# Graph attention and mixture of experts: the one-hot rows of the edge counts written in the order in which TensorE reads them

## The reference

```
xn = layernorm(x); h = xn @ W + b_w
e = leaky_relu(s_dst[dst] + s_src[src] + b_a);  w = exp(e)
out = segment_sum(w / denom[dst] * h[src], dst);  x = x + out
x = x + moe(layernorm(x))        # 8 experts, top 2, gelu
```

## Time and profile before

| | us |
|---|---|
| median of 3 runs | 788.67 (786.93 to 788.84) |
| profiled execution, its time | 787.67 |
| its span, first to last instruction | 786.0 |
| PE busy | 701.5 |
| DVE busy | 559.3 |
| ACT busy | 458.8 |
| POOL busy | 283.5 |

### The profile page before, as it was taken

The page is one execution under the profiler, slowest core; times in us unless marked ns, Lnnn a source line. Parts: engine busy times, 40 slices in busy tenths (PEclk is TensorE's granted clock), DMA queues, the critical chain, the costliest instruction groups (busy, mean ns, idle before and its releaser), DMA issues.

```text
span 786.0 us, 15439 instructions
## 1 busy us (share of the span) xinstructions
PE 701.5 (89%) x3556; PEld 527.0 (67%) x3557; DVE 559.3 (71%) x1520; ACT 458.8 (58%) x1226; POOL 283.5 (36%) x427
## 2 busy tenths in 40 slices
PE   3977863999899999999999999999589899999992
PEld 1855641777677776767677777776347788888881
DVE  4999977999888898879887888853495333333331
ACT  3223379778778776767676777721354455555551
POOL 3336620022222222222111222211305677777764
PEclk9888976999999999999999999999789999999998
DMA  9431000000000000000000000000793577777766
GB/s 337 158 107 55 0 1 1 15 29 28 28 27 3 28 27 28 27 28 27 28 27 28 27 12 17 27 28 28 245 407 112 103 130 133 133 128 135 135 119 80
DMA packets 28949, 59.70 MB, mean 76 GB/s; under 512 B 3664, under 2 KB 8144, under 8 KB 28624
## 3 DMA queue, kind: packets, MB, share of 16 engines
q0 software_dynamic: 10176, 24.12, 17.1%
q1 hardware_dynamic: 18704, 34.89, 12.0%
HBM read 35.93 MB, written 23.07 MB: 75 GB/s over the span
## 4 chain that ended last, share of the span: by engine, by line
PE 52%; DMA 10%; issue 5%; DVE 4%; POOL 2%; POOLq 2%; ACT 0%; DVEq 0%; ACTq 0%
PE ps L772 10%; PE ps L790 10%; PE ps L773 9%; DMA out_dram<-y,si 9%; PE ps L726 7%; PE ps L879 3%; PE ps L753 2%; PE ps L893 2%; PE ps L737 2%; PE ps L820 1%; DMA xg<-xn_table,gi 1%; PE ps L746 1%; PE ps L869 1%; PE ps L759 1%; DVE hot_r L1509 1%
## 5 line engine op out<-in xcount | busy, mean ns | idle before, releaser
L973 ACT ACTIVATE weight<-sdst_b,ss 128x125 f32 (+1 forms) x400 | 118.3, 386 | 95.5 <-DVE A_lo L1339 95.5
L772 PE MATMUL ps<-H_hi,A_hi 128*125 128x512 f32 x400 | 163.0, 408 | 0.9 <-DVE x_all L1353 0.9
L773 PE MATMUL ps<-H_lo,A_hi 128*125 128x512 f32 x400 | 157.9, 395 | 0.0
L1278 DVE TENSOR_SCALAR hot_k<-lane_k,key_t 128x250 bf16<-128x250 bf16 x600 | 120.6, 282 | 4.4 <-DVE weight_sum L1327 4.3
L524 POOL TENSOR_SCALAR seed<-seed 128x1 f32<-128x1 f32 x20 | 4.2, 210 | 330.9 <-DVE seed L1380 330.9
L982 ACT ACTIVATE weight<-weight,ss 128x125 f32<-128x125 f32 x400 | 119.8, 384 | 0.0
L790 PE MATMUL ps<-H_hi,A_lo 128*125 128x512 f32 x400 | 104.9, 402 | 0.0
L726 PE MATMUL ps<-hot_k,hot_l 128*128 128x250 bf16 x500 | 80.7, 286 | 16.0 <-DVE hot_k L1278 15.9
L772 PEld LDWEIGHTS ps<-H_hi,A_hi 128*125 128x125 f32 x400 | 74.2, 185 | 21.6 <-issue 3.7
L773 PEld LDWEIGHTS ps<-H_lo,A_hi 128*125 128x125 f32 x400 | 74.3, 186 | 16.1
L879 PE MATMUL ps<-W_e,xgT 128*128 x352 | 85.0, 385 | 0.0
(11 more groups left out here) (235 smaller groups left out, 1126.7 us busy)
## 6 DMA issues: line engine op xcount, KB each, us to landing
W_e<-in_L_ffn_W_dram SPq DMA_DIRECT2D x16, 512.0 KB, 9.3
xf<-in_x_cols_dram SPq DMA_DIRECT2D x10, 512.0 KB, 5.9
x_all<-in_x_dram SPq DMA_DIRECT2D x20, 256.0 KB, 5.8
out_dram<-x_all SPq DMA_DIRECT2D x20, 256.0 KB, 2.0
xn_table<-xn SPq DMA_DIRECT2D x20, 256.0 KB, 2.2
b_b<-in_L_ffn_b_dram SPq DMA_DIRECT2D x1, 2048.0 KB, 12.6
Wf<-in_L_gnn_W_dram SPq DMA_DIRECT2D x1, 1024.0 KB, 5.5
out_dram<-x_all POOLq DMA_DIRECT2D x4, 256.0 KB, 7.8
```

Source lines behind the costliest of these rows:

```text
L772: pe.matmul(ps_agg[0:TN, :], A_hi[:, k, :], H_hi[:, k, :], start=(k == 0), stop=False)
L773: m = pe.matmul(ps_agg[0:TN, :], A_hi[:, k, :], H_lo[:, k, :], start=False, stop=False)
L973: m = nc.scalar.activation(weight[:, s, k, :], dst_scores, ACT.Relu, bias=ss[:, 0, k:k + 1], scale=1.0 - SLOPE)
L1278: return nc.vector.tensor_scalar(into, lane_k[:, :], float(HW * h), key, ALU.add, ALU.is_equal)
```

## The change

Four edits go together.

- `hot_l` has HALVES * BASE + 1 = 31 matrices in place of 19. Matrix BASE * h + c belongs to chunk c of half h, as in `hot_k`. TensorE reads it at a fixed address and loads one word of the table instead of eleven.
- `pair_rows` is called once per half, inside `pairs_of`, right ahead of that half's three `hot_k`. It writes three matrices (384 elements) and reads the source lanes at an address from registers (`at + rel`). The one call per tile between two folds is gone.
- In steps where t is a register (those of the loop) `count` waits once, for the tenth half of the tile; in the steps written out it waits for each half as before.
- `hot_l` grows by 12 * 256 bytes per partition. To make room, small tensors of the table's setup now share places with others; their operations are the same.

```diff
-            regs = [pe.alloc_register(f"pe_word{k}") for k in range(WORDS - 1)]
+            regs = [pe.alloc_register("pe_word")]
...
-                chunk = [pe.snap(within(pe.snap(regs[h]), 0, SPAN - BASE)) for h in range(HALVES)]
                 def low_of(h, c):
-                    return hot_l[:, bass.ds(chunk[h] + c, 1), :].rearrange("p c n -> p (c n)")
+                    return hot_l[:, BASE * h + c, :]
...
+                at_once = not isinstance(t, int)
+                if at_once:
+                    pe.wait_ge(pairs_ok, HALVES * t + HALVES)
                 for h in range(HALVES):
-                    pe.wait_ge(pairs_ok, HALVES * t + h + 1)
+                    if not at_once:
+                        pe.wait_ge(pairs_ok, HALVES * t + h + 1)
...
-            def pair_rows(at):
-                shape = [P, SPAN, P // 2, 2]
+            def pair_rows(h, chunk):
+                shape = [P, BASE, P // 2, 2]
                 return nc.vector.tensor_tensor(
-                    hot_l[:, 0:SPAN, :].rearrange("p c (n j) -> p c n j", j=2),
+                    hot_l[:, BASE * h:BASE * h + BASE, :].rearrange("p c (n j) -> p c n j", j=2),
                     lane_l[:, :].rearrange("p (n j) -> p n j", j=2).unsqueeze(1).to_broadcast(shape),
-                    lo2[:, bass.ds(at, SPAN), :].unsqueeze(2).to_broadcast(shape), ALU.is_equal)
+                    lo2[:, bass.ds(chunk, BASE), :].unsqueeze(2).to_broadcast(shape), ALU.is_equal)
...
                     rel = dve.snap(within(dve.snap(regs[1 + h]), 0, SPAN - BASE))
+                    pair_rows(h, dve.snap(within(at + rel, 0, CW - BASE)))
                     for c in range(BASE):
                         m = hot(hot_k[:, BASE * h + c, :], h, key_t[:, bass.ds(rel + c, 1)])
...
                     fold(t + 1, 1 - s, 1)
-                    if has(t, -2):
-                        pair_rows(at)
                     for n in range(2, 5):
```

More of the change, by code:

```diff
@@ L120, in gnn_moe_kernel @@
         layer_end = top[0]
+        lo_n = sg("lo_n", [1, BANKS * NT, 2], F32, layer)
+        ex_n = sg("ex_n", [1, BANKS * NT, 2], F32, layer)
+        rel_n = sg("rel_n", [1, NT, HALVES], F32, layer)
+        ex_t = sg("ex_t", [1, 3, NT], F32, layer)
+        zero_t = sg("zero_t", [1, NT], F32, layer)
+        thr = sg("thr", [P, 2, 2], F32, layer)
+        found = sg("found", [P, 2, 2], F32, layer)
+        chunk_mm = sg("chunk_mm", [P, 2, CG], F32, layer)
+        layer_end = top[0]
         layer.close()
@@ L126, in gnn_moe_kernel @@
         A_lo = sg("A_lo", [P, NT, TN], F32R, first)
-        hot_l = sg("hot_l", [P, SPAN + 1, P], BF16, first)
+        hot_l = sg("hot_l", [P, HALVES * BASE + 1, P], BF16, first)
         weight_sum = sg("weight_sum", [P, 2, TN], F32, first)
@@ L131, in gnn_moe_kernel @@
         reach("stage_1_end", max(layer_end, top[0]), first)
-        chunk_mm = sg("chunk_mm", [P, 2, CG], F32, first)
         thr_i = sg("thr_i", [P, 2], I32, first)
[L134 to L140, removed]
         ss = sg("ss", [P, 2, NT], F32, first)
@@ L727, in count @@
                                   start=(h % 2 == 0 and c == 0), stop=False)
-                more = extra_in(pe, regs[HALVES])
+                more = extra_in(pe, regs[0])
                 with pe.If(more > 0):
-                    at = pe.snap(extras_before(pe, regs[HALVES]) * HALVES)
+                    at = pe.snap(extras_before(pe, regs[0]) * HALVES)
                     with pe.Fori(0, more) as n:
@@ L733, in count @@
                             pe.wait_ge(xpair_ok, at + n * HALVES + h + 1)
-                            pe.matmul(half_of(h), hot_l[:, SPAN, :], hot_k[:, HALVES * BASE, :],
+                            pe.matmul(half_of(h), hot_l[:, HALVES * BASE, :], hot_k[:, HALVES * BASE, :],
                                       start=False, stop=False).then_inc(xcount_ok, 1)
@@ L1297, in pairs_of @@
                                                     tile_key[:, bass.ds(t, 1)], None, ALU.subtract).then_inc(xkey_ok, 1)
-                            nc.vector.tensor_tensor(hot_l[:, SPAN, :], lane_l[:, :],
+                            nc.vector.tensor_tensor(hot_l[:, HALVES * BASE, :], lane_l[:, :],
                                                     lo2[:, bass.ds(chunk, 1), 0].to_broadcast([P, P]), ALU.is_equal)
@@ L1426, in _ @@
             first_at = pair_keys(0)
-            pair_rows(first_at)
             dve.wait_ge(key_ok, 1)
```

## The result

The changed kernel takes 812.11 us (median of 4 runs, 811.61 to 812.87) against 788.46 of before: ratio 1.0304, 95% interval [1.0287, 1.0322]. It is slower, as forecast, and 9 us above the 803 forecast. The stated range of 794 to 813 holds it by 0.9 us; rival 1's own range, 797 to 809, does not. The profiled execution took 811.65 us with a span of 810.0, against 787.67 and 786.0.

What follows compares the result with a forecast made beforehand. TensorE bounds the loop now, VectorE after the change (1.7 us more a tile): +6.8 ahead, +0.4 at step 3, +8.3 in the loop, -0.5 behind sum to +15.0 us on 787.67, giving 803; range 794 to 813.

Steps and rivals of the forecast that it cites:

- rival 1: Whole kernel: VectorE becomes the bound, 803 us, own range 797 to 809; chance 0.78.
- VectorE becomes the bound, so the kernel gets slower: Loop: VectorE's new round of 44.6 us exceeds TensorE's 40.6, adding 8.3 us; the kernel goes to 803.
- the room of 1.9 us a round: Loop before the change: VectorE's work and jump pause take 41.16 of 43.04 us, leaving 1.9, not 4.6.
- rival 2: Loop: VectorE's 2.9 us pause ahead of even steps is room and can shrink; 787 us, not slower; chance 0.07.
- 1.49 us a tile for ten small instructions: VectorE's pair_rows: ten instructions cost 2.75 us, the one removed saves 1.26; net +1.49 us a tile.
- The 0.18 for the fold and the address: VectorE, per tile: lost overlap between two folds, 0.08 us, plus the first new instruction's address computation, 0.1 us.
- The pause ahead of even steps, 2.9 us as before: VectorE's jump back: pause stays 2.9 us, six times 2.91 in the loop; its shrinking would prove the forecast wrong.
- I count nothing: TensorE's clock: new pauses up to 3 us in even steps priced at zero, since 2 us idle kept 2.4 GHz.
- The sum: Whole kernel: 6.8 before step 3, 0.4 there, 8.3 in the loop, -0.5 behind it; +15.0 us.
- rival 3: Loop's odd steps: the count's single wait makes weigh wait, 0.6 us in each of 7, +4: 807; chance 0.07.
- the idle ahead of odd steps: Sign in the loop's profile: VectorE's idle there, 1.66 us before, would be gone, under 0.3 us.
- The counts at 2.9 us: TensorE in the loop: 25 count matmuls fall from 4.33 (even) and 3.90 us (odd) to near 2.9.

Runs made afterwards that it cites:

- e6: The changed kernel with VectorE's loop alone written out, so without its jump back: 782.05 us, ratio 0.9923 to the kernel before.
- e7: The kernel before with VectorE's loop alone written out, so without its jump back: 788.22 us, ratio 0.9996.
- e2: The changed kernel with the reciprocal, which raises den_ok, moved ahead of the first five halves of one-hots: 786.39 us, ratio 0.9992 to the kernel before.
- e1: The changed kernel with extra, never-read matmuls filling TensorE's pause ahead of the product that waits for den_ok: 797.41 us, ratio 1.0128 to the kernel before.
- e5: The kernel before with nothing but the single wait per tile in the loop's count: 783.20 us, ratio 0.9933.
- e4: The changed kernel with TensorE computing the same hot_l addresses from registers, as before: 807.19 us, ratio 1.0266 to the kernel before.
- e3: The changed kernel with a wait for each half in the loop, as before: 807.97 us, ratio 1.0257 to the kernel before.
- e12: The kernel before with pair_rows called a second time per tile, two folds later (1.26 us more on VectorE): 819.82 us, ratio 1.0411.
- e9: The kernel before with the loops of VectorE and TensorE both written out: 771.92 us, ratio 0.9785.

## Why the prediction was right, and where it was not

- *VectorE becomes the bound, so the kernel gets slower:* right. e6 and e7 show the jump's pause as VectorE's own, and with it the room of 1.9 us a round; rival 2 falls as a whole, though the pause did shrink by 0.7 us, which the prediction had named as a sign against itself.
- *1.49 us a tile for ten small instructions:* right; 352 ns each against 359. Step 2 grew by 1.58 us (1.7 forecast), the loop's even step by 20.73 - 19.40 = 1.33 and the odd by 20.39 - 18.85 = 1.54 (L1358 to the end of the last hot_k, from 264.33, 286.77 and 309.31 less their idle). The 0.18 for the fold and the address is thus not seen in the loop. The Trainium skill's price, an estimate of 357 ns by "VectorE: DVE Perf Modes", section "The TRN2 errata — SBUF-src ops pay a fixed extra latency per instruction", is met by this trace too.
- *The pause ahead of even steps, 2.9 us as before:* too long. It is 2.2 us in five of six rounds; the jump itself is no shorter, but more work is queued when it is taken (e2). VectorE's round alone is thus 43.5 us (e1), not the 44.6 of the sum: 0.7 by the pause, and the rest by the steps, 41.1 in place of 41.65.
- *"I count nothing" for the clock:* the step that failed. The prediction saw the pauses of up to 3 us at this wait (L759, now L763), took the 2 us of step 3 as proof that the clock stays, and priced them at zero. Even these 2 us were PEld's; PE's own pause at 206.03 us was 1.52. The new pauses cost 1.8 us a round (45.26 against 43.46): 12.6 us in the loop's six waits, and 2.9 at step 3. That is 15.5, nearly all of it the clock's: e1 gave back 14, after the 1.7 that its own matmuls cost.
- *The sum:* 24.0 against 15.0. In the loop 13.2 against 8.3: 12.6 for the waits behind the slow clock, less 7 * (44.6 - 43.5) = 7.7 for VectorE's shorter round. Ahead of it 9.5 against 7.2, the difference at step 3; behind it 0.5 against -0.5; and the 0.8 of the first stage. The forecast was as near as it was because two errors in the loop had opposite signs. That is luck, and so is the place inside the range: its upper end came from rival 3, which did not happen. Of the signs that it gave for itself, the idle ahead of odd steps did not go and the pause ahead of even steps did not stay.
- *The counts at 2.9 us:* right (2.87). That fixed addresses give all of it was wrong: e5 shows that most of the gain, 0.8 of 1.45 and of 1.02 us, is the work for the waits. The prediction had the single wait down as a risk alone; on the kernel before it is a gain by itself (e5). No run has the fixed addresses with the old hot_l, since they need its new order.
- *Rival 3, weigh waits for the counts:* not in the changed kernel (the trace of the loop has no such wait), and in e4 as soon as the counts are slow.

The Trainium skill, "TensorE: Matmul & The Clock Gate", section "HAM oscillation — how this bites in real kernels", describes a like failure, with waits for DMA in the place of this wait for VectorE: pauses between groups of matmuls let the clock fall, and each group then starts at half rate. The traces agree that it happens: 0.50 behind 3.1 us of idle, 1.00 behind 0.9 us. Between these the same pause had either outcome, in the changed kernel and e3 behind 2.5 us, in e2 and e12 behind 1.5 to 2.6.

## What to carry to other kernels

When a change lengthens the engine that is not the bound, look at what the bound engine does while it waits: a wait in the middle of its work can be followed by a lower clock, as here, and the slow stretch comes back as a wait on the other side. Raise early the semaphore that such a wait stands on. And price each edit of a change alone: here one wait in place of ten gave 0.7% by itself, and with the other edits beside it the kernel was 3.0% slower.

## What the runs showed of the hardware

- A jump back cost VectorE's sequencer 2.8 to 3.1 us and TensorE's 0.2. The engine was idle for less of it where it had more work left at the branch: 2.9 us with 0.3 us of work left (before), 2.5 with 1.0 (one round of the changed kernel; 2.2 in the others), 1.1 with 2.1 (e2).
- A pause of 2.5 us once left TensorE's clock at 1.00 and once not, in the same code. In e12 it fell behind 1.50 us and stayed behind 2.39. Behind 3.0 to 3.2 us it fell each time, twelve times in the changed kernel and e3.
- 25 matmuls of 250 bf16 columns took 2.88 us with nothing in their way, 2.9 to 3.2 with one register operation each where the loop is written out (e9), 3.1 to 3.5 with it in the loop (e5), and 3.9 to 4.4 with a wait for each half too (before).
